# Two-layer graph kernel: x for the first residual loaded from DRAM, and the last MLP of the first layer wholly in fp32r parts

## What is computed

```python
def _cxin_conv(x, a, eps, W, b):
    ax = a @ x
    h = ax + (1.0 + eps[0]) * ax
    for i in range(3):
        h = relu(h @ W[i].T + b[i])
    return h
# layer 0
out1, out2 = _cxin_conv(x, adj, eps1, W1, b1), _cxin_conv(x2, adj, eps2, W2, b2)
x = _layernorm(x + concatenate((out1, out2), axis=1) @ Wm.T + bm)
# layer 1
A_hat = adj + eye(4096)
d = rsqrt(sum(A_hat, axis=1))
x = _layernorm(x + (d[:, None] * A_hat * d[None, :] @ x) @ W.T + b)
```

## Time and profile before

| what | value |
|---|---|
| three runs, median | 592.26 us (591.4 to 592.6) |
| the profiled execution, its own time | 591.38 us |
| its span, first to last instruction | 589.6 us |
| PE busy | 583.0 us (99%) |
| DVE busy | 545.4 us (93%) |
| ACT busy | 378.8 us (64%) |
| POOL busy | 28.1 us (5%) |
| mean granted TensorE clock | 0.998 of full speed |

### The profile page before, as it was taken

One profiled execution on the slowest core, in us unless ns is written; L12 is line 12 of the kernel. 1 busy time (PEld: TensorE's weight loads), 2 busy tenths in 40 slices (PEclk: granted clock), 3 DMA queues, 4 the chain that ended last, 5 costly groups with the idle time before them and its releaser, 6 DMA issues.

```text
span 589.6 us, 7659 instructions
## 1 busy us (share of the span) xinstructions
PE 583.0 (99%) x2676; PEld 485.9 (82%) x2676; DVE 545.4 (93%) x695; ACT 378.8 (64%) x512; POOL 28.1 (5%) x26
## 2 busy tenths in 40 slices
PE   9999999999999999999999999999999999999996
PEld 8888888888888888888888888878888888888885
DVE  6999999998988998898799999997999997989986
ACT  6544437852454773453667336479799799799794
POOL 0000000001100000110000020000200001010011
PEclk9999999999999999999999999999999999999999
DMA  8968565443655544354544374776899999999921
GB/s 330 397 248 294 206 223 206 145 148 143 207 196 179 179 169 145 142 197 178 195 147 143 143 268 187 261 287 222 316 365 392 425 377 340 387 338 367 387 77 72
DMA packets 31131, 141.91 MB, mean 241 GB/s; under 512 B 5504, under 2 KB 6272, under 8 KB 17024
## 3 DMA queue, kind: packets, MB, share of 16 engines
q1 hardware_dynamic: 30528, 139.87, 64.6%
q10 hardware_dynamic: 576, 1.70, 0.7%
HBM read 139.40 MB, written 2.16 MB: 240 GB/s over the span
## 4 chain that ended last, share of the span: by engine, by line
PE 97%; ACT 1%; DVE 1%; issue 1%; POOLq 0%; POOL 0%; DVEq 0%
PE ps L536 81%; PE pd L557 6%; PE ps L612 6%; PE pd L566 2%; PE pd L598 1%; PE pd L664 1%; ACT outn L756 0%; ACT ahi L723 0%; DVE z L1217 0%; ACT ahi_extra L723 0%; DVE stats L1222 0%; POOLq L124 0%; POOL rstd L1246 0%; DVE mv L1007 0%; DVE vareps L1014 0%
## 5 line engine op out<-in xcount | busy, mean ns | idle before, releaser
L723 ACT ACTIVATE ahi<-raw 128x1024 fp32r<-128x1024 f32 x212 | 222.6, 1060 | 162.5 <-PE ps L536 156.3
L920 DVE TENSOR_TENSOR alo<-raw,ahi 128x1024 fp32r<-128x1024 f32 x212 | 256.5, 1218 | 27.0 <-ACT ahi L723 26.0
L536 PE MATMUL ps<-ahi,x2s 128*128 128x512 f32 x512 | 138.4, 389 | 0.0
L536 PE MATMUL ps<-ahi,x1hi 128*128 128x512 f32 x384 | 121.9, 393 | 0.0
L536 PE MATMUL ps<-ahi,x1lo 128*128 128x512 f32 x384 | 120.9, 390 | 0.0
L536 PE MATMUL ps<-alo,x1hi 128*128 128x512 f32 x384 | 120.6, 390 | 0.0
L536 PEld LDWEIGHTS ps<-ahi,x2s 128*128 128x128 f32 x512 | 96.4, 188 | 20.1
L536 PEld LDWEIGHTS ps<-alo,x1hi 128*128 128x128 f32 x384 | 72.2, 188 | 15.1
L536 PEld LDWEIGHTS ps<-ahi,x1lo 128*128 128x128 f32 x384 | 72.3, 188 | 15.0
L536 PEld LDWEIGHTS ps<-ahi,x1hi 128*128 128x128 f32 x384 | 71.9, 188 | 15.0 <-issue 0.7
L536 PE MATMUL ps<-alo,x2s 128*128 128x512 f32 x256 | 80.2, 389 | 0.0
(11 more groups left out here) (103 smaller groups left out, 526.6 us busy)
## 6 DMA issues: line engine op xcount, KB each, us to landing
raw<-a_t SPq DMA_DIRECT2D x108, 1024.0 KB, 4.9
raw<-a_t SPq DMA_DIRECT2D x32, 512.0 KB, 7.4
raw<-early SPq DMA_DIRECT2D x7, 512.0 KB, 7.5
xn<-x SPq DMA_DIRECT2D x2, 1024.0 KB, 7.8
xn<-x SPq DMA_DIRECT2D x3, 512.0 KB, 10.5
out<-outn ACTq DMA_DIRECT2D x3, 512.0 KB, 6.6
par<-params SPq DMA_DIRECT2D x1, 708.0 KB, 12.4
raw<-head SPq DMA_DIRECT2D x2, 256.0 KB, 3.1
```

What stands on the lines that cost most here:

```text
L536: mm = pe.matmul(ps[bank + (CH * (q % 2) if layer else 0)][:, :], block_of(w, n), a[c], start=(n == 0 and k == 0), stop=(n == JB - 1 and k ...
L723: act.activation(ring_hi(layer, q, n), raw_tile(layer, n), ACT.Copy).then_inc(hi_ready, 1)
L920: dve.tensor_tensor(ring_lo(layer, q, n), raw_tile(layer, n), as_f32(ring_hi(layer, q, n)), ALU.subtract).then_inc(lo_ready, 1)
```

## The change

The last MLP (plan 1) does its first dense layer as three fp32r products too. ACT rounds the evacuated `h` (four instructions), DVE writes its rest (four more). All of plan 1's steps are placed later: dense layers after tiles 4, 6 and 8 (were 1, 3 and 5), the merge after tile 10 (was 6), ReLUs at 7, 9 and 10 (were 4, 6 and 7); what follows the merge moves by four steps (`DVE_RESIDUAL`, `DVE_AGGREGATE`, `DVE_SHIFT` and what is counted from them), `last_y` from 20 to 24, `split_y` of the last quarter from 25 to 29, the last `xn` from 29 to 32. DVE's `split_h` in plan 1 goes two pieces at a step.

For `xb`, SP loads x from a new DRAM input `rows` (512 KB a quarter) once the residual before has been taken; `residual_base` is gone in all four quarters, and `residual_bias` waits for the load. In the last quarter it stands at step 25 (was 20 and 21 for the two).

```diff
-PE_DENSE = ({3: 0, 5: 1, 8: 2}, {1: 0, 3: 1, 5: 2})
-PE_MERGE = (10, 6)
-DVE_SPLIT_H = {4: 1, 6: 2}
+PE_DENSE = ({3: 0, 5: 1, 8: 2}, {4: 0, 6: 1, 8: 2})
+PE_MERGE = (10, 10)
+DVE_SPLIT_H = {3: (0, 0), 4: (0, 2), 5: (1, 0), 6: (1, 2), 8: (2, 0), 9: (2, 2)}
...
-ACT_RELU = ({k + SPLIT: l for k, l in PE_DENSE[0].items()}, {4: 0, 6: 1, 7: 2})
+ACT_RELU = ({k + SPLIT: l for k, l in PE_DENSE[0].items()}, {7: 0, 9: 1, 10: 2})
...
-ACT_NORM_LAST = 29
+ACT_NORM_LAST = 32
-DVE_BASE_LAST = 20
+DVE_BASE_LAST = 25
-ACT_NORM = (22, 20)
+ACT_NORM = (22, 24)
-DVE_MAKE_Y = (KB + 4, 2 * KB + 4, 3 * KB + 3, 23)
+DVE_MAKE_Y = (KB + 4, 2 * KB + 4, 3 * KB + 3, 27)
...
+            def load_base(q):
+
+                if not (isinstance(q, int) and q == 0):
+                    sp.wait_ge(z_ready, q)
+                src = rows[q] if isinstance(q, int) else rows[bass.ds(q, 1)].rearrange("o p w -> (o p) w")
+                sp.dma_start(xb[:, :, :], src.rearrange("p (k d) -> p k d", d=P)).then_inc(xb_in, 16)
...
+                    if i == 3:
+                        load_base(q)
...
+            load_base(0)
             with sp.Fori(1, QUARTERS - 1) as q:
...
                 load0(groups - 1, s)
+                if s == 0:
+                    load_base(LAST)
...
-                    elif l:
-                        wait(pe, hlo_ready, q * (LAYERS * M) + (M * (l - 1) + m + 1))
+                    else:
+                        wait(pe, hlo_ready, q * (LAYERS * M) + (M * l + m + 1))
                         passes = ((whi, hhi), (whi, h_rest), (wlo, hhi))
-                    else:
-                        wait(pe, h_ready, q * (4 * M) + (M * l + m + 1))
-                        passes = ((par, h),)
...
-                if plan == 0 and n in (ACT_EVACUATE[0] + 1, ACT_EVACUATE[0] + 2):
+                if n in (ACT_EVACUATE[plan] + 1, ACT_EVACUATE[plan] + 2):
                     for m in range(CH):
-                        round_h(q, 0, CH * (n - ACT_EVACUATE[0] - 1) + m)
+                        round_h(q, 0, CH * (n - ACT_EVACUATE[plan] - 1) + m)
...
-            def residual_base(q):
-
-                dve.tensor_tensor(xb[:, :, :], as_f32(quarter(x1hi, q)), as_f32(quarter(x1lo, q)),
-                                  ALU.add).then_inc(xb_step, 1)
-
             def residual_bias(q):
 
-                wait(dve, xb_step, q + 1)
+                wait(dve, xb_in, q * 16 + 16)
...
                         if p in DVE_SPLIT_H:
-                            for m in range(M):
-                                split_h(LAST, DVE_SPLIT_H[p], m, 1)
+                            l, first = DVE_SPLIT_H[p]
+                            for m in range(first, first + CH):
+                                split_h(LAST, l, m, 1)
```

More of the change, by code:

```diff
@@ L120, with build @@
 X_AFTER = {1: 1, 3: 2, 5: 3, 8: 4, 13: 5, 20: 6}
-def build(nc, a_t, head, early, x12, params, scratch, out):
+def build(nc, a_t, head, early, x12, rows, params, scratch, out):
     with ExitStack() as ctx:
@@ L216, in build @@
         merge_done = sem("merge_done")
-        xb_step = sem("xb_step")
+        xb_in = sem("xb_in")
         xb_ready = sem("xb_ready")
@@ L940, in split_h @@
                     wait(dve, h_ready, q * (4 * M) + (M * l + m + 1))
-                wait(dve, hhi_ready, q * (LAYERS * M) + (M * (l - plan) + m + 1))
+                wait(dve, hhi_ready, q * (LAYERS * M) + (M * l + m + 1))
                 dve.tensor_tensor((hlo, h_rest)[plan][:, m, :], h[:, m, :], as_f32(hhi[:, m, :]),
                                   ALU.subtract).then_inc(hlo_ready, 1)
-            def residual_base(q):
-                dve.tensor_tensor(xb[:, :, :], as_f32(quarter(x1hi, q)), as_f32(quarter(x1lo, q)),
-                                  ALU.add).then_inc(xb_step, 1)
             def residual_bias(q):
-                wait(dve, xb_step, q + 1)
+                wait(dve, xb_in, q * 16 + 16)
                 dve.tensor_tensor(xb[:, :, :], xb[:, :, :], bias_rows(BM_AT), ALU.add).then_inc(xb_ready, 1)
@@ L1034, in mlp_step @@
                 if plan == 0 and n == DVE_BASE:
-                    residual_base(q)
-                if plan == 0 and n == DVE_BASE + 1:
                     residual_bias(q)
@@ L1143, in layer0_quarter @@
                         if n == DVE_BASE_LAST:
-                            residual_base(q)
-                        if n == DVE_BASE_LAST + 1:
                             residual_bias(q)
@@ L1302 @@
                                for i, (q, k0, k1) in enumerate(X_PIECES)]),
+        "rows": np.ascontiguousarray(x["x"].reshape(QUARTERS, P, QW)),
         "params": params,
```

## The result

The changed kernel takes 592.74 us (median of 22 runs) beside 591.42 us for the kernel before on the same chip. One run of each took far longer and is left out of the ratio. The ratio is 1.0022, with a 95% interval of 1.0017 to 1.0028: 1.3 us slower, at the edge of what I had called measurable, and three to four times the +0.35 us of the sum. The profiled execution took 593.52 us, with a span of 591.7 us. It reached its first dense layer at 104.69 us where the profile before has 103.93; the profiles of the experiments have 103.5 to 104.3, and 103.92 in `base_late`, which does the same as the changed kernel up to far behind that place.

A forecast was written before the change was run, and what follows sets the result against it. PE, busy 99% of the span, was taken to bound the kernel, with DVE nearest to making it wait. Terms -0.71 + 0.70 + 0.35 + 0 = +0.35 us on a base of 592.26 gave 592.6 us, range 591.1 to 594.0.

The forecast's parts named there:

- the sum: Whole kernel: PE's saving, two PE waits in the last MLP and zero elsewhere, netting +0.35 us.
- no others: Sign in the changed profile: PE idles once before tile 4's and once before tile 6's `alo` products, nowhere else.
- PE's work, -0.71: Last MLP's first dense layer: fp32 at 3.43 us becomes fp32r at 2.72, saving PE 0.71 us on the path.
- PE 0.7 less busy: Sign in the changed profile: PE's total busy time falls by 0.7 us.
- x from DRAM, 0: Residual: loads hidden, cost 0; dropped adds gain nothing directly, but the fourth puts DVE 1.14 us earlier.
- Rival (d): Residual's new load not hidden, or holding up tile loads: DVE waits at step 10 or 25; 0.17 shared with another rival.
- Tile 4, 0.70: Last MLP: two new DVE halves ahead of tile 4 make its `alo` late, so PE stands 0.7 us.
- tile 6, 0.35: Last MLP: DVE's next-layer halves, waiting for ACT's ReLUs, make tile 6's rest late; PE stands 0.35 us.
- The queue after the merge, 0: Tiles 11 to 32: DVE and ACT deliver just in time with no reserve, costing PE 0.
- Rival (c): Late queue breaks at tiles 22 to 31 through POOL or ACT: 0.5 to 1.3 us more, middle 593.5; chance 0.13.
- the forecast: Main case: PE's saving outweighed by waits at tiles 4 and 6, net -0.1 to +0.9 us; chance 0.52.
- (a): Last MLP: no PE wait appears, so PE's saving stays whole, 591.55 us; chance 0.18.

The follow-up runs named there:

- base_late: Changed kernel with one DVE add (second layer's base, last quarter) moved from tile 92 to tile 112; 592.67 us, ratio 1.0024.
- x_only: Kernel before with only x loaded from DRAM for the residual and the bias add at step 25, MLP as before; 591.43 us, ratio 1.0001.
- replaced: Changed kernel with dense layers after tiles 3, 5, 8, merge after 11, ReLUs at 6, 8, 12, a layer's four halves at one step; 591.51 us, ratio 1.0008.
- mlp_only: Changed kernel with x summed from its two parts again at steps 20 and 21, MLP as changed; 593.66 us, ratio 1.0040.
- both_fixed: Kernel `replaced` with layer 1's variances and shifts one tile earlier and the four identities before tile 97 no longer in a row; 591.34 us, ratio 1.0000.
- relu_11: Changed kernel with ACT doing the last dense layer's four ReLUs after rounding tile 11 instead of tile 10; 592.82 us, ratio 1.0022.

## Why the prediction came out as it did

The time lay in the range and in the class that I gave the most chance, and the 592.6 us stand 0.1 from the measured median. That nearness is luck. The base of 592.26 was the median of three runs; 22 runs of the kernel before have 591.42, so the base was 0.84 us too high, and the sum was 0.97 too low. Of the +1.3 us the sum had only +0.35, its own upper bound was a net of +0.9, and its sign "no others" of the holes failed.

- **PE's work, -0.71.** Right. The three dense layers are 2.72 us each where nothing disturbs them, and `replaced` has the saving whole. The sign "PE 0.7 less busy" was wrong, since PE's rows cover part of its holes.
- **x from DRAM, 0.** Right: `x_only` at 1.0001. That the 1.14 us of the fourth add matter was right too: `mlp_only` pays 0.9 to 1.1 us without them. Rival (d) is out.
- **Tile 4, 0.70, and tile 6, 0.35.** The places and releasers were right, the sizes 0.63 and 0.27. What the terms lacked is that PE loses more than it stands: a pair of product matmuls behind such a wait took 0.74 us, not 0.61. Tile 4 ended 0.76 us late (397.82 against its start, 395.54, and 1.36, and the 0.16 by which a row outlasts the next start), tile 6 0.41. 1.17 in all against 1.05.
- **The queue after the merge, 0.** This step failed. Up to tile 31 it was right: the least spare time is 0.31 us, at tile 30 (the prediction had 0.05), and there is no hole. But "So 0, with no reserve" ended the walk at place 32, and I took for settled that DVE is ahead from there on. It meets the work of the next quarters with 0.9 us less than before, and tiles 95 and 97 spend it: +0.61 us, and tile 127 adds 0.19. Rival (c) had the mechanism, a late queue that breaks, and a size of 0.5 to 1.3, but looked at tiles 22 to 31 alone.
- **The two cases that I weighed against each other**, the forecast and (a), both lived in the MLP. (a) is out in the changed kernel, but `replaced` shows that the waits were a matter of the steps' places and not of the added work: its MLP is as (a) wanted it, 591.5 us.

No version here beats the kernel before by what can be measured: `both_fixed` at 1.0000 and `replaced` at 1.0008 are level with it, 1.2 to 1.4 us better than the changed kernel. PE's saving is real, but in every version that has it DVE and ACT made PE wait again later. At tile 127 PE waited for DVE even before the change: it took that `alo` 190.12 us after tile 0's start, in `replaced` 190.23 and in `both_fixed` 190.02 us after it.

## What to carry to other kernels

When an edit delays a helper engine that already works without a pause, follow its lead to the place where that lead is smallest in the whole program, not to the end of the edited stage: here, as far as the rows above show it, the lead lost near tile 11 was spent 120 us later. Measure it as spare time, tile by tile, before and after; it shows a loss long before a wait does. But take it at each tile that may be late: `base_late` had more of it at tile 93 and was still late at tile 95, where ACT was the late engine. And an idle gap of an engine that is not the bound, such as DVE's 2.0 us behind ACT's ReLUs, is worth looking at when work is queued behind it with no slack.

## What the runs showed of the hardware

- A semaphore wait costs PE more than the time it stands. In the changed kernel's trace the first pair behind one took 0.74 us from start to end, where others took 0.61 to 0.62; a single matmul took 0.50 where others took 0.39. That is 0.11 to 0.13 us a wait, 0.5 us at the four waits at tiles 4, 6, 95 and 97.
- In the added loads 512 KB landed in 5.6 us in the median.
- The first rounding of a tile by ACT behind ReLUs from PSUM has a record of 1.17 to 1.21 us where others have 1.06. This is part of what `relu_11` had not reckoned with: DVE started 1.23 us after that rounding's start, not 1.0.
